# A two-layer graph network on one core: one block from the weighting to the edge stage, and the stages before it laid out anew

## What is computed

```python
h = relu(layernorm(x))                                   # layer 0: attention over edges
z = (h @ W).reshape(N, 4, 32)
alpha = leaky_relu(s_src[src] + s_dst[dst], 0.2)         # s = z with att, per head
ex = exp(alpha - m[src])                                 # m: max over the edges of src, at least 0
denom = segment_sum(ex, src) + (E - deg)[:, None] * exp(-m)
w = ex / denom[src]
x = x + segment_sum(w[:, :, None] * z[dst], dst) + bias
h = relu(layernorm(x))                                   # layer 1: an MLP over edges
msg = relu(concat(h[src], h[dst], edge_attr) @ W1 + b1) @ W2 + b2
out = x + segment_sum(msg, src)
```

## Time and profile before

| | us |
|---|---|
| runs | 5880.04, 5880.95, 5888.17; median 5880.95 |
| profiled execution, its own time | 5881.77 |
| its span in the profile | 5880.0 |
| PE, DVE, ACT, POOL busy | 4392.8, 3805.5, 2408.9, 3336.3 |
| scatter, 1568 indirect stores on POOL | 968 ns each |
| edge stage, 1664 gathers on POOL | 1017 ns each |

### The profile page before, as it was taken

One profiled execution on the slowest core, in us unless ns is written; L12 is line 12 of the kernel. 1 busy time (PEld: TensorE's weight loads), 2 busy tenths in 40 slices (PEclk: granted clock), 3 DMA queues, 4 the chain that ended last, 5 costly groups with the idle time before them and its releaser, 6 DMA issues. The chain is left out here.

```text
span 5880.0 us, 110731 instructions
## 1 busy us (share of the span) xinstructions
PE 4392.8 (75%) x23630; PEld 3470.2 (59%) x23827; DVE 3805.5 (65%) x7129; ACT 2408.9 (41%) x3697; POOL 3336.3 (57%) x3490
## 2 busy tenths in 40 slices
PE   3668777777777777202999947888888888888886
PEld 3556666666666666202888824666666666666665
DVE  7665444444444444188999856777777777777774
ACT  2435555555555545113666612333333333333332
POOL 1227777777777777700000004777777777777772
PEclk9988888888888888656999979999999999999998
DMA  9836555565555555990000044555555555555556
GB/s 256 339 96 154 139 141 140 141 141 140 142 138 141 142 142 140 60 54 0 0 0 0 6 112 129 139 137 140 140 139 139 140 139 139 137 142 139 139 137 96
DMA packets 1028261, 725.54 MB, mean 123 GB/s; under 512 B 763114, under 2 KB 845860, under 8 KB 1028108
## 3 DMA queue, kind: packets, MB, share of 16 engines
q1 hardware_dynamic: 685580, 387.14, 29.8%
q0 software_dynamic: 131616, 276.04, 17.3%
q10 hardware_dynamic: 211040, 62.08, 4.4%
HBM read 563.04 MB, written 161.88 MB: 123 GB/s over the span
## 5 line engine op out<-in xcount | busy, mean ns | idle before, releaser
L1140 POOL DMA_INDIRECT g_q<-q_d,g_rec x1664 | 1692.0, 1017 | 1612.2 <-DMA g_lrow<-low_row_d 1110.9
L594 POOL DMA_INDIRECT rec_d<-rec,place x1568 | 1517.8, 968 | 517.3 <-issue 515.4
L1257 PE MATMUL g_hp<-pw,g_mix 128*128 x3328 | 937.2, 404 | 299.8 <-DVE g_q L1166 267.3
L1221 ACT ACTIVATE g_hid<-g_q 128x512 f32<-128x512 f32 x832 | 523.7, 629 | 1508.1 <-DVE g_q L1166 1169.4
L1177 DVE TENSOR_TENSOR agg<-agg,g_ap 128x256 f32 x1664 | 697.6, 419 | 576.9 <-PE g_ap L1268 350.2
L679 PE MATMUL lk<-tab_sd,low 128*128 128x196 f32 x3136 | 1055.5, 424 | 0.0
L1257 PEld LDWEIGHTS g_hp<-pw,g_mix 128*128 128x128 f32 x3328 | 565.4, 189 | 665.5 <-issue 621.6
L627 DVE TENSOR_REDUCE rank<-equal 128x4 f32<-128x512 bf16 x392 | 262.1, 684 | 1006.2 <-ACT equal L571 980.7
L1268 PE MATMUL g_ap<-g_hid,g_oh 128*128 128x256 f32 x3328 | 878.4, 387 | 30.7 <-DVE agg L1177 11.4
L676 PE MATMUL lk<-mask,hx 122*128 122x245 bf16 x1568 | 481.7, 307 | 423.3 <-ACT low L560 423.3
L1268 PEld LDWEIGHTS g_ap<-g_hid,g_oh 128*128 128x128 f32 x3328 | 599.1, 190 | 181.8 <-issue 109.7
(11 more groups left out here) (231 smaller groups left out, 4754.7 us busy)
## 6 DMA issues: line engine op xcount, KB each, us to landing
low_row<-rows_d SPq DMA_DIRECT2D x392, 256.0 KB
rec_d<-pad SPq DMA_DIRECT2D x64, 936.0 KB, 5.6
g_rec<-rec_d SPq DMA_DIRECT2D x208, 288.0 KB
rec<-in_ea ACTq DMA_DIRECT2D x196, 256.0 KB
hx_row<-rows_d SPq DMA_DIRECT2D x392, 98.0 KB
g_lrow<-low_row_d SPq DMA_DIRECT2D x208, 128.0 KB
g_q<-q_d,g_rec POOLq DMA_INDIRECT x1664, 2.8
rec_d<-rec,place POOLq DMA_INDIRECT x1568
```

Of the source, the lines that this page charges most:

```text
L594: pool.indirect_dma_start(rec_d, bass.IndirectOffsetOnAxis(ap=place[0:n, at, j:j + 1], axis=0), rec[0:n, at, j, :], None).then_inc(s_sc[at ...
L1140: pool.indirect_dma_start(qg[:, par, j, :], None, q_d, bass.IndirectOffsetOnAxis(ap=rec[:, par, j, F_IDX:F_IDX + 1].bitcast(I32), axis=0)) ...
L1221: act.activation(hid[:, u, :, :], qg[:, par, 2 * u:2 * u + 2, :], ACT.Relu).then_inc(s_hid, 1)
L1257: mm = pe.matmul(hp[u][:, k * HID:(k + 1) * HID], mix[:, par, 2 * u + k, :], pw[:, bass.ds(b[k], 1), :].rearrange("p o f -> p (o f)"), sta ...
```

## The change

- The host passes src and dst by partition. In the counting, five loads go to ACT's queue, the casts of digits to ACT, the store of `rows_d` ahead of the fill loop, the square into xs, hb one iteration ahead.
- The base block is gone: base is made at the start of the scatter, head_i at its end, blk in the softmax beside the scatter of heads (iota on POOL, products on PE).
- Softmax: most arrays are laid into pw and agg. The logs and their Exp go head by head into whole rows (`line`), in pairs of heads.
- Weighting, layer 1's node part and the edge stage are one block. The weighting has four buffers (`quads`). POOL adds the bias to x in five chunks (5, 8, 12, 12, 12 blocks). The loads of x, h, the weights and the first two groups stand ahead of the loop. The norm goes by chunks; a chunk's six steps lie between the blocks of the chunk before. ACT makes hb; PE turns block b + 1 ahead of the products of b; q is stored by SP, x2 in chunks by ACT; agg is cleared half by DVE, half by ACT.
- Edge stage: the records are loaded in two pieces (64 attributes; 4 floats with digits and index), the turned one-hot is made on ACT as relu(1 - |row - p|) in four operations a group, two tiles go per transpose at u = 0, and the plain one-hot is eight operations of 128 x 128.

The diff, cut to its core:

```diff
-    src_v, dst_v = (a.rearrange("(g p j) -> p g j", p=P, j=G) for a in (src, dst))
+    src_v, dst_v = (a.rearrange("(p g j) -> p g j", p=P, j=G) for a in (src, dst))
...
+            sp.wait_ge(s_row, 2)
+            sp.dma_start(rows_d.rearrange("r (p c) -> p r c", p=P), rows[:, :, :]).then_inc(s_rowst, 16)
...
+            v.tensor_scalar(bits[:, 4, :], s_of, 15, None, ALU.bitwise_and).then_inc(s_fb, 1)
+            v.wait_ge(s_attl, 32)
...
+            v.wait_ge(s_in, 16)
             link(v.tensor_reduce(st[:, 0, :], xs[:, :, :], X, ALU.add))
...
+            v.wait_ge(s_dstl, 16)
...
+            onehot(0, 0)
+            v.wait_ge(s_std, 1)
+            v.reciprocal(st[:, 1, :], st[:, 0, :]).then_inc(s_rstd, 1)
+            onehot(1, 1)
+            with v.Fori(1, NG // 2) as i:
+                onehot(i * 2, 0)
+                onehot(i * 2 + 1, 1)
...
+            act.dma_start(flat_i[:, 0, :], src_t.rearrange("(p c) -> p c", p=P)).then_inc(s_flat, 16)
+            act.dma_start(wx[:, 0:D], W).then_inc(s_attl, 16)
+            act.dma_start(attb[:, :, :, :].rearrange("p h s c -> p (h s c)"),
+                          att.rearrange("o h c -> o (h c)").to_broadcast([P, 2 * HEADS * OC])).then_inc(s_attl, 16)
+            act.dma_start(flat_i[:, 1, :], dst_t.rearrange("(p c) -> p c", p=P)).then_inc(s_flat, 16)
+            act.dma_start(dst_i[:, :, :], dst_v).then_inc(s_dstl, 16)
...
+            def normed(it):
                 act.activation(hb[:, :], cent[:, bass.ds(it, 1), :].rearrange("p o d -> p (o d)"), ACT.Relu,
                                scale=st[:, 1, bass.ds(it, 1)]).then_inc(s_h, 1)
+
+            def step(it, last=False):
                 moved(it, 0)
                 act.wait_ge(s_t, it + 1)
                 if not first(it):
                     act.wait_ge(s_mm, it)
                 act.activation(hT[:, :], tp[:, 0:P], ACT.Copy).then_inc(s_hT, 1)
+                if not last:
+                    normed(it + 1)
...
+            pool.iota(low_in[:, :], [[1, TILES]], base=0, channel_multiplier=0).then_inc(s_pi, 1)
...
+                act.activation(high_dst[:, at], fld[:, at, DHIGH], ACT.Copy).then_inc(s_ld, 1)
...
-            for h in range(HEADS):
-                act.wait_ge(s_dn, h + 1)
-                act.activation(hd[:, :, h], sc[:, h, :], ACT.Ln).then_inc(s_ln, 1)
-            for h in range(HEADS):
-                act.wait_ge(s_ln, h + 1)
-                act.activation(hd[:, :, h], hd[:, :, h], ACT.Exp, scale=-1.0).then_inc(s_r0, 1)
+            for pair in ((0, 1), (2, 3)):
+                for h in pair:
+                    act.wait_ge(s_dn, h + 1)
+                    act.activation(line[h], sc[:, h, :], ACT.Ln).then_inc(s_ln, 1)
+                for h in pair:
+                    act.wait_ge(s_ln, h + 1)
+                    act.activation(line[h], line[h], ACT.Exp, scale=-1.0).then_inc(s_r0, 1)
...
-                link(v.tensor_tensor(fld[:, :, h], sc[:, h, :], hd[:, :, h], ALU.mult))
-                link(v.scalar_tensor_tensor(out=sc[:, h, :], in0=fld[:, :, h], scalar=2.0, in1=hd[:, :, h],
+                link(v.tensor_tensor(line[HEADS], sc[:, h, :], line[h], ALU.mult))
+                link(v.scalar_tensor_tensor(out=sc[:, h, :], in0=line[HEADS], scalar=2.0, in1=line[h],
...
+        for bs in chunk:
+            pool.tensor_tensor(x2[:, bs, :], x2[:, bs, :], row(bias_b[:, :], P, bs.stop - bs.start, D), ALU.add).then_inc(s_xb0, 1)
+        pool.wait_ge(s_qs[0], 16 * (NB - NB // 2))
+        pool.wait_ge(s_qs[1], 16 * (NB // 2))
+        pool.wait_ge(s_pm, NB)
...
 
     @block.vector
     def _(v):
-        v.memset(agg[:, :, :], 0.0).then_inc(s_az, 1)
-        v.wait_ge(s_az, 1)
-
...
+        def weigh(g, at):
+            tile = lambda a: a[:, bass.ds(g * G, G)]
+            if not first(g, 4):
+                v.wait_ge(d_acc, g - 3)
...
+        for step in range(6):
+            normalise(0, step)
...
+        for c in range(NC):
+            for i in range(SIZES[c]):
+                b = chunk[c].start + i
+                v.scalar_tensor_tensor(out=x2[:, b, :], in0=b2_b[:, :], scalar=deg[:, b:b + 1], in1=x2[:, b, :],
+                                       op0=ALU.mult, op1=ALU.add).then_inc(s_xb, 1)
+                for step in range(6):
+                    if c + 1 < NC and step * (SIZES[c] - 3) // 5 == i:
+                        normalise(c + 1, step)
+                v.wait_ge(s_p, b + 1)
+                v.tensor_tensor(pw[ED:P, 2 * b:2 * b + 2, :], pp[b % 2][ED:P, :].rearrange("p (s f) -> p s f", s=2),
+                                row(b1_b[ED:P, :], BLK, 2, HID), ALU.add).then_inc(s_pm, 1)
...
-            js = slice(half * HG, (half + 1) * HG)
-            v.tensor_tensor(oh[:, par, js, :], rec[:, par, js, F_LOW:F_LOW + 1].to_broadcast([P, HG, P]),
-                            row(iota[:, :], P, HG, P), ALU.is_equal).then_inc(s_oh, 1)
+            for j in range(half * HG, (half + 1) * HG):
+                ins = v.tensor_scalar(oh[:, par, j, :], iota[:, :], aux[:, par, j, 0:1], None, ALU.is_equal)
+            ins.then_inc(s_oh, 1)
...
+                if not last and u >= 2:
+                    if u == 2:
+                        v.wait_ge(s_ix[1 - par], (g + par) * 8 + 16)
+                    onehot(g + 1, 1 - par, u - 2)
...
+        def turned_low(g, at):
+            if not first(g, 4):
+                act.wait_ge(d_acc, g - 3)
+            for j in range(HG, G):
+                ins = act.activation(oh_low[:, at, j, :], iota[:, :], ACT.Abs, bias=low_dst[:, bass.ds(g * G + j, 1)], scale=-1.0)
+            ins.then_inc(d_dist, 1)
+            act.wait_ge(d_dist, g + 1)
+            act.activation(oh_low[:, at, HG:G, :], oh_low[:, at, HG:G, :], ACT.Relu, bias=ones[:, 0:1], scale=-1.0
+                           ).then_inc(d_lo, 1)
...
+                act.wait_ge(s_t, b + 1)
+                if b >= 2:
+                    act.wait_ge(s_p, b - 1)
+                act.activation(hT[:, b % 2, :], tp[b % 2][:, 0:P], ACT.Copy).then_inc(s_hT, 1)
+                if c + 1 < NC and 3 * (SIZES[c] - 3) // 5 + 1 == i:
+                    square(c + 1)
+                if c + 1 < NC and 4 * (SIZES[c] - 3) // 5 + 1 == i:
+                    root(c + 1)
+                if b + 2 < NB:
+                    normed(b + 2)
+                act.wait_ge(s_qr, b + 1)
+                if b >= 2:
+                    act.wait_ge(s_qs[b % 2], b // 2 * 16)
+                act.activation(qrow[:, b % 2, :], qp[b % 2][:, 0:HID], ACT.Copy).then_inc(s_qm, 1)
+                if c and i == 1:
+                    act.wait_ge(s_xb, ENDS[c - 1])
+                    act.dma_start(x2_d[chunk[c - 1].start * P:ENDS[c - 1] * P, :].rearrange("(b p) d -> p b d", p=P),
+                                  x2[:, chunk[c - 1], :]).then_inc(s_xs, 16)
+        act.wait_ge(s_xb, NB)
+        act.dma_start(x2_d[chunk[NC - 1].start * P:NB * P, :].rearrange("(b p) d -> p b d", p=P),
+                      x2[:, chunk[NC - 1], :]).then_inc(s_xs, 16)
...
         def turned(g, par, k):
-            act.wait_ge(s_tp, g * 2 + (k + 1))
+            act.wait_ge(s_tp, g + 1)
             if k == 0 and not first(g, 2):
                 act.wait_ge(s_hp, (g - 1) * PG)
-            act.activation(mix[0:ED, par, HG * k:HG * (k + 1), :].rearrange("p j e -> p (j e)"),
-                           tp[k][0:ED, :], ACT.Copy).then_inc(s_eaT, 1)
+            act.activation(mix[0:ED, par, k:G:2, :], tp[par][k * ED:(k + 1) * ED, :].rearrange("p (j e) -> p j e", j=PG),
+                           ACT.Copy).then_inc(s_eaT, 1)
+
+        def distance(g, par, half):
+            if half == 0:
+                act.wait_ge(s_lr[par], (g - par) * 8 + 16)
+            cols = slice(half * HG * P, (half + 1) * HG * P)
+            act.activation(mix[ED:P, par, half * HG:(half + 1) * HG, :].rearrange("p j q -> p (j q)"),
+                           lrow[ED:P, par, cols], ACT.Abs, bias=minus[ED:P, 0, 0:1]).then_inc(s_dist, 1)
+
+        def turned_onehot(g, par, half):
+            act.wait_ge(s_dist, g * 2 + (half + 1))
+            at = mix[ED:P, par, half * HG:(half + 1) * HG, :].rearrange("p j q -> p (j q)")
+            act.activation(at, at, ACT.Relu, bias=one_col[ED:P, 0:1], scale=-1.0).then_inc(s_ohT, 1)
...
-                if u >= 2 and not last:
-                    turned(g + 1, 1 - par, u - 2)
-
+                if not last:
+                    if 1 <= u < 3:
+                        turned_onehot(g + 1, 1 - par, u - 1)
+                    if u < 2:
+                        distance(g + 1, 1 - par, u)
+                if 1 <= u < 3 and not last:
+                    turned(g + 1, 1 - par, u - 1)
...
+        turn_block(0)
+        for b in range(NB):
+            if b + 1 < NB:
+                turn_block(b + 1)
+            if b >= 2:
+                pe.wait_ge(s_qm, b - 1)
+            pe.wait_ge(s_hT, b + 1)
```

(22 more changed lines are left out.)

598 lines of the change are left out of this document (277 added, 321 removed).

## The result

The changed kernel takes 5692.16 us (median of 4 runs, 5684.69 to 5694.40), the kernel before 5882.29 beside it: a ratio of 0.9673, 95% interval 0.9662 to 0.9684. It is 190 us faster; 5657 was forecast, 35 less, and the time lies inside the range. The profiled execution took 5691.81 us, with a span of 5690.0.

A forecast was written before the change was run, and what follows sets the result against it. No engine bounds the whole; each stage has its own limit, with joins between. Terms -27 - 24 - 21 - 25 - 106 - 21 = -224 from 5880, plus 1, gave 5657 us, range 5590 to 5720.

The forecast's parts named there:

- Counting, gap, softmax: Stages before the weighting, scatter aside: counting and prologue -27 us, gap between counting loop and scatter -24, softmax -21.
- the 5.15: Last 16 counting iterations: DVE is next late, 5.15 us an iteration, -11 us.
- PE's own floor is 596.15 / 208 = 2.87: Weighting: with four buffers PE is next late, 2.88 us a group; -25 us in all.
- POOL's adds: Weighting: POOL adds the bias to x beside it; some 4 us lost, 27 if all its time hit DVE.
- 85 us in all: Block loop: DVE's total with the norm's passes, next after PE; 49 blocks at 1.87 plus 3 give 95 us.
- 24 us: Way from weighting to edge stage: loads gone from there, now under the weighting; part of that stretch's -106 us.
- DVE's adds wait 6.6 us in all ... so POOL does not hold it: Edge stage: DVE's adds wait little, 3.9 us of it for gathers, so POOL is not the limit.
- Rival 1: Edge stage falls to POOL's rate, near 10.1 us a group, without the long one-hot: 83 us more gain, 5574; chance 0.1.
- the ring: Edge stage: PE and DVE block-number reads in a 5.25 us two-step loop set 10.5 a group; change gains 21 us.
- Rival 4: Edge stage: short one-hots come onto the path, 0.96 us a group, 200 us, giving 5857; chance 0.03.
- Rivals 2: Edge period stays or grows to 10.6 to 10.75 us, adding 21 to 52, giving 5695; chance 0.18.
- 5: Slower: ACT becomes the edge stage's engine, 11.7 us a group, giving 5907; chance 0.04.

The follow-up runs named there:

- experiments 1: Changed kernel with 64 bytes instead of 4 a row for the array `last`, shifting the scatter's arrays; 7148.27 us, 0.9611 of the kernel before, on a slow chip.
- 10: Changed kernel with PE's block-number reads ahead of the wait, bias added on DVE, `last` laid into `wgt`; 7064.65 us, 0.9591 of the kernel before, slow chip.
- Experiment 2: Changed kernel with two buffers instead of four in the weighting; 7216.83 us, one run, on a slow chip.
- Experiment 3: Changed kernel with the bias added to x by DVE in each chunk, not by POOL; 7175.81 us, 0.9645 of the kernel before, on a slow chip.
- experiment 6: Changed kernel with all chunks of the norm ahead of the block loop instead of between its blocks; 5697.32 us, one run.
- experiment 7: Changed kernel with six chunks (5, 6, 8, 10, 10, 10 blocks) instead of five; 5695.64 us, 0.9696 of the kernel before.
- experiment 5: Changed kernel with the edge stage's plain one-hots as long 128 x 512 operations instead of four of 128 x 128; 5675.62 us, one run.
- 8: Changed kernel with fixed block numbers in the edge stage, so PE and DVE read none into registers; 5582.31 us, one run.
- 12: Changed kernel with PE's block-number reads ahead of the wait, bias on DVE, `last` in `wgt`, on a normal chip; 5585.61 us, 0.9514 of the kernel before.

## Why the prediction was right, and where it was not

**Counting, gap, softmax: right.** The first product came at 55.16 for a forecast of 56.5. The last 16 iterations are 5.24 apart (5.79 before, by the transposes), DVE 73.87 busy in 82.70 us: next late was DVE, for whose one-hots PE waits 32 times in this stretch, as the step said, and it is 0.09 above the 5.15. The softmax's logs and Exp on rows:

```profile
2668.02 1.59 ACT L777 ACTIVATE agg<-pw 128x1664 f32<-128x1664 f32 x1 [0.27 <-DVE pw L840]
2669.63 1.28 ACT L780 ACT_TABLE_LOAD   x1
2670.92 3.07 ACT L780 ACTIVATE agg<-agg 128x1664 f32<-128x1664 f32 x2
2672.60 1.89 DVE L899 TENSOR_TENSOR agg<-pw,agg 128x1664 f32<-128x1664 f32 x1 [0.89 <-issue]
```

Each number is the one taken from the earlier trace rows; DVE's twelve steps run without a gap from 2672.60 to 2695.7.

**Scatter: a cost of 16 us that no term held.** The part was taken at nothing because its instructions are the same. All 1568 stores are 10 to 13 ns longer; the gathers are not. Shifted addresses on the chip (experiments 1 and 10) don't bring it back, and the kernel before has the short stores on the slow chip too. The cause is open; the loads of the integers by partition, the layout of `rows_d` and the longer program weren't tried one by one.

**Weighting: right mechanism, wrong floor.** The step "PE's own floor is 596.15 / 208 = 2.87" failed. It took a busy time as a floor, and with it the wrong engine as next late. DVE's own work, which the same paragraph has as 2.8, was the floor: 2.781. A product has a mean of 336 ns in both traces, but the records of products overlap (3328 x 0.336 would be 1118 us), and where PE stops less within a group more of them do: 578.64 us busy for what had been 596.15. With DVE as the bound the sum would have been 628.2 - 208 x 2.8 = 46: the measured gain is 46.5. Experiment 2 shows that it was the buffers.

**POOL's adds: the loss fell elsewhere.** They were costed at up to 4 us and, at worst, 27, with the loss on DVE. In the changed kernel DVE lost nothing, POOL everything: 552 us for one operation, and the four others came behind the stage, 10.6 us of the join. In experiment 2 the loss was where the prediction had it: the adds took 17.8 us, and the stage 17 us more than in the kernel before. The Trainium skill (SBUF — State Buffer, Who interferes with whom) says that a DVE instruction with two SBUF inputs contends with a GpSimd one that reads SBUF, and of the shared ports that whoever issues first has them for the whole instruction while the other fully blocks; the traces agree, DVE's operations being held in experiment 2 and POOL's in the changed kernel, and the latter goes beyond it in that some 590 operations of DVE (three a group from 2724 to 3275) went first. Experiment 3 takes the adds away and the join falls by 9.6 us.

**Block loop: two errors of opposite sign.** The steady block was forecast at 1.87 and is 1.70: 8 us too much. But the step counted the chunks' work only in DVE's total ("85 us in all", under PE's 92), as if it could be spread at will. It is a line of steps with ACT's square among them, which holds ACT's copies, and PE, the bound, doesn't make up what it loses. And the loads ("24 us", gone) were counted without the one that the change leaves at the end of the weighting, beside which the stores of q are late. Together they are at most the 23 to 28 us of experiment 6, which doesn't tell them apart; experiment 7 shows that smaller portions alone don't lower them. Join 17.6 + loop 110.2 + 14.2 to the first add, and 4.8 from the last multiply to the copy, is the 146.8 of the table; forecast were 7.5 + 95 + 11.

**Edge stage: the size right, its reason not shown; what holds the changed kernel is.** The gain is 0.087 us a group for a forecast of 0.1. But the step "DVE's adds wait 6.6 us in all ... so POOL does not hold it" looked at DVE's waits alone. Behind the first three groups POOL has only three pauses over 0.35 us in the kernel before, and 8 x (1.017 + 0.318) = 10.68 us is the period from add to add there (2219.6 / 207.75): POOL was full too. In the changed kernel it has 139 such pauses, which are 113 us beyond the usual 0.3. The kernel before stood at both limits at once, and no run tells whether the 0.087 came from the wait taken off PE, as forecast, or from gathers that are 65 ns shorter. Nor is it well clear of the spread: three kernels with the same code in this stage (the changed one, experiments 6 and 7) take 2199 to 2212 us in it. Rival 1 (the period falls to POOL's rate once the long one-hot is gone) fell even so: the ring keeps it near 10.6, and experiment 5 gets the same stage time with that one-hot. But its number was right as the next limit: with the reads gone (8) or moved (12) the stage goes to 10.14 and 10.15, where rival 1 put 10.1. Rival 4 fell: by experiment 5 the eight short one-hots cost DVE 0.40 us a group, not its 0.96, since four in line overlap, and the kernel nothing:

```profile
4204.20 0.87 DVE L1076 TENSOR_SCALAR g_oh<-iota,g_aux 128x128 f32<-128x128 f32 x4
```

The Trainium skill (VectorE: DVE Perf Modes, on the TRN2 errata) says that every instruction with SBUF sources pays a fixed latency. The trace agrees, 0.87 us for four where one long one takes 0.68, and the price isn't on the ring. Rivals 2 and 5 didn't come: ACT is busy 1338.91 of 2195.10 us, 61%.

**The sum.** Forecast too good by 28.5 on the way to the edge stage, 16.4 in the scatter, 3.5 ahead of it, 3 in the edge stage, 3.7 behind it and 0.7 in the softmax; too cautious by 21.5 in the weighting. That is 34 of 224 us, and the runs' median lies the 35 above 5657.

## What to carry to other kernels

A read into a register that stands between a wait and the product it addresses is on the path even where every engine looks idle: look for "issue" once a step in front of the same instruction, and put the read ahead of the wait (93 us here). Don't give POOL an operation with two inputs beside a stage in which DVE runs such operations back to back: here it didn't run until DVE was done, and with two buffers it ran and held DVE for as long. A busy time is not an engine's floor while it still waits in the middle of a group; where two are both near full, take each one's work without its waits, and only then the larger. And before an engine is ruled out as a limit, look at its own pauses, not only at who waits for it: POOL had none in the edge stage of the kernel before.

## What the runs showed that was not expected

- One POOL add of 640 elements a row recorded at 552.165 us beside DVE's two-input operations, and 12.4 us for four larger ones without them. With two buffers the same five adds took 17.8 us, and DVE's operations beside them up to 5.00 instead of 1.78.
- Indirect stores of one form are 958 ns (median) in the kernel before and 967 to 971 in every kernel made from the changed one, on every chip used.
- There are chips on which the large loops stand still for 2 to 4 us at a time (5870 us becomes 7430), with single instructions and the smaller loops as fast as elsewhere. A gain of 93 us in the edge stage can't be read off there.
- The edge stage of experiment 7 is 13 us longer than that of its neighbours, though only chunk sizes ahead of it differ.
